# Fifteen list scatters in each attention pass and eighteen in the drain pass, with 31 left for the shared tiles

## The reference

```
xn = layernorm(x);  q, k, v = split(xn @ w_qkv);  q, k = elu(q) + 1, elu(k) + 1
kv[t] = decay * kv[t-1] + k[t] * v[t];  ks[t] = decay * ks[t-1] + k[t]
x = x + ((q * kv) / max(sum_d(q * ks), 1e-6)) @ w_out
```

```
xn2 = layernorm(x);  logits = xn2 @ router_w.T + router_b;  top 4 of 32
x = x + sum_4 share_e * down_e(silu(gate_e(xn2)) * up_e(xn2)) + shared(xn2)
```

## Time and profile before

| | us |
|---|---|
| median of 3 executions | 738.56 (735.03 to 739.55) |
| the profiled execution | 739.91 |
| its span, first to last instruction | 737.8 |
| PE busy in the span | 607.2 (82%) |
| DVE busy | 478.2 (65%) |
| ACT busy | 463.4 (63%) |
| POOL busy | 439.0 (59%) |

### The profile page before, as it was taken

The page is one execution under the profiler, slowest core; times in us unless marked ns, Lnnn a source line. Parts: engine busy times, 40 slices in busy tenths (PEclk is TensorE's granted clock), DMA queues, the critical chain, the costliest instruction groups (busy, mean ns, idle before and its releaser), DMA issues.

```text
span 737.8 us, 15716 instructions
## 1 busy us (share of the span) xinstructions
PE 607.2 (82%) x4797; PEld 419.7 (57%) x4797; DVE 478.2 (65%) x1894; ACT 463.4 (63%) x1118; POOL 439.0 (59%) x367
## 2 busy tenths in 40 slices
PE   4999988898897825576999999999999999999100
PEld 2467656566564413354777776777776777777000
DVE  2469979898896615444766666666666666666063
ACT  2687757677664203455877777877777777878100
POOL 3122287687687573444038787778878778887400
PEclk9999999999999966888999999999999999999655
DMA  9865788888756663566558887888888888887799
GB/s 290 295 179 161 234 242 255 284 248 251 241 162 207 214 205 100 185 203 203 167 135 139 136 146 139 138 136 147 137 144 140 136 140 138 144 142 97 162 412 379
DMA packets 122419, 140.41 MB, mean 190 GB/s; under 512 B 23586, under 2 KB 111170, under 8 KB 121794
## 3 DMA queue, kind: packets, MB, share of 16 engines
q1 hardware_dynamic: 89776, 97.29, 44.0%
q0 software_dynamic: 29040, 38.68, 29.6%
q10 hardware_dynamic: 3522, 3.44, 1.5%
HBM read 79.19 MB, written 64.89 MB: 195 GB/s over the span
## 4 chain that ended last, share of the span: by engine, by line
PE 65%; DVE 11%; another core or an unknown queue 6%; issue 5%; DMA 4%; ACT 3%; SPq 2%; POOL 2%; ACTq 0%; POOLq 0%; DVEq 0%
PE psD L1250 13%; PE psQ L1217 13%; PE psK L1217 12%; PE psT L1188 6%; PE psK L1266 3%; PE psV L1266 3%; SPq L513 2%; PE psT L1237 2%; PE psV L1237 2%; DMA W<-acc_scratch 2%; PE psD L1310 2%; PE psQ L1266 2%; DVE W L878 2%; DVE stats L806 1%
## 5 line engine op out<-in xcount | busy, mean ns | idle before, releaser
L637 POOL DMA_INDIRECT acc_scratch<-arena x159 | 249.3, 1568 | 96.6 <-DMA acc_scratch<-arena 42.8
L585 POOL DMA_INDIRECT xlist_scratch<-list_row,dest x128 | 134.9, 1054 | 66.6 <-issue 34.2
L1041 DVE COPY arena<-psT 128x512 f16<-128x512 f16 x191 | 81.1, 425 | 111.1 <-PE psT L1188 73.9
L1250 PE MATMUL psD<-W,arena 128*128 (+1 forms) x955 | 137.8, 276 | 8.1 <-DVE arena L1037 8.1
L1217 PE MATMUL psQ<-W,arena 128*128 (+1 forms) x570 | 111.2, 332 | 23.5 <-DVE arena L1041 17.9
L1217 PE MATMUL psK<-W,arena 128*128 (+1 forms) x576 | 112.2, 332 | 6.6 <-issue 4.7
L1250 PEld LDWEIGHTS psD<-W,arena 128*128 128x128 f16 x955 | 86.4, 99 | 15.7 <-DVE arena L1037 8.3
L1217 PEld LDWEIGHTS psQ<-W,arena 128*128 128x128 f16 x570 | 51.1, 99 | 57.6 <-DVE arena L1041 18.0
L669 ACT ACTIVATE arena<-arena 128x192 f16<-128x192 f32 x191 | 69.2, 362 | 16.3 <-DVE arena L1065 5.1
L1188 PE MATMUL psT<-ident,arena 128*128 128x128 f16 x764 | 75.4, 222 | 3.1 <-issue 3.0
L1188 PEld LDWEIGHTS psT<-ident,arena 128*128 128x128 f16 x764 | 58.1, 99 | 33.6 <-issue 12.4
(11 more groups left out here) (174 smaller groups left out, 1090.1 us busy)
## 6 DMA issues: line engine op xcount, KB each, us to landing
arena<-xlist_scratch SPq DMA_DIRECT2D x159, 136.0 KB
W<-acc_scratch SPq DMA_DIRECT2D x24, 512.0 KB, 12.8
acc_scratch<-arena SPq DMA_DIRECT2D x16, 512.0 KB, 6.8
arena<-in_L_attn_x_dram SPq DMA_DIRECT2D x10, 512.0 KB, 5.3
arena<-in_L_ffn_down_w_dram SPq DMA_DIRECT2D x23, 192.0 KB
xlist_scratch<-pad_scratch SPq DMA_DIRECT2D x32, 136.0 KB
list_row<-xrow_scratch SPq DMA_DIRECT2D x32, 136.0 KB
acc_scratch<-arena SPq DMA_DIRECT2D x33, 128.0 KB, 8.0
```

Of the source, the lines that this page charges most:

```text
L585: nc.gpsimd.indirect_dma_start(xlist[:, :], bass.IndirectOffsetOnAxis(ap=dest[:, n:n + 1], axis=0), list_row[j % LISTS][:, :], None).then_ ...
L637: nc.gpsimd.indirect_dma_start(acc[t % ACCS][:, :], bass.IndirectOffsetOnAxis(ap=token[:, (t - NT) % DEEP:(t - NT) % DEEP + 1], axis=0), y ...
L1041: nc.vector.tensor_copy(xT[t % 2].rearrange("p s c t -> p (s c t)"), psX[t % 2]).then_inc(xT_done, 1)
L1250: last = nc.tensor.matmul(psY[u], aT[u][0:height, part], weights(t - 2, GUW + q * H, H, height), start=(n == 0), stop=(n == len(parts) - 1))
```

## The change

It moves ten scatters into passes 3 to 7, two for each, so that the drain pass begins with n = 79 in place of 69. The drain pass does eighteen in place of twenty, and 31 in place of 39 are left. In the order of POOL's pass, the group between the two roots grows from four to five, and the group behind the second root from five to six; all others keep their size. `FETCHED` becomes 1, 2, 6, 10, 14, 17, 21, 26 for b = 2 to 9, before it was 1, 2, 6, 9, 12, 15, 19, 24. In the shared tiles SP therefore loads row tiles 26 and 27 at tiles 0 and 2, where it loaded 24 to 27 at tiles 0, 2, 5 and 7; the last four come at tiles 10, 12, 15 and 17 as before. No tile loads anything at 5 and 7 now.

```diff
-        LIST_FROM = [0, 0, 0] + [4 + 13 * n for n in range(NB - 2)] + [89]
+        LIST_FROM = [0, 0, 0] + [4 + 15 * n for n in range(NB - 2)] + [97]
...
+        def late_list(t):
+
+            j = NT - TS + (t - 10) // 5 * 2 + t % 5 // 2 if t >= 10 else FETCHED[NB + 1] + t // 5 * 2 + t % 5 // 2
+            return j if t % 5 in (0, 2) and j < (NT if t >= 10 else NT - TS) else None
...
-                if t % 5 in (0, 2) and FETCHED[NB + 1] + t // 5 * 2 + t % 5 // 2 < NT:
-                    load_list(FETCHED[NB + 1] + t // 5 * 2 + t % 5 // 2)
+                if late_list(t):
+                    load_list(late_list(t))
...
                 if b >= 3:
-                    list_some(2, 6)
+                    list_some(2, 7)
                 if st.now:
                     k_sum_product(b)
                 if st.before:
                     root(1, b - 1)
                 if b >= 3:
-                    list_some(6, 11)
+                    list_some(7, 13)
                 if st.now:
                     kv_sum_product(b, 0)
                 if b >= 3:
-                    list_some(11, 12)
+                    list_some(13, 14)
                 if st.now:
                     kv_sum_product(b, 1)
-                list_some(12 if b >= 3 else 0, 20)
+                list_some(14 if b >= 3 else 0, 20)
```

## The result

The kernel after takes 738.19 us (median of 20 runs, 733.23 to 746.2), the kernel before on the same chip 736.04 us (20 runs, 727.5 to 743.82). The ratio is **1.0075, interval 1.0043 to 1.0106**. It compares only executions within 1.5% of the fastest of their kernel, here 19 of after's and 12 of before's, while the medians of all twenty differ by 0.29%, so the size of the loss on this chip is less sure than the interval looks. The forecast was 732.6 us. On another chip, where before takes 683.47 us, after takes 692.23: **1.0135, interval 1.0101 to 1.0168**.

A forecast was written before the change was run, and what follows sets the result against it. Bounds: waits through DVE, PE and ACT in the passes, and holes on scatter trains in the shared tiles. 7.1 - 3.8 - 9.3 = -6.0 us from 739.91 gave 733.9; allowing for its 1.35 above the median, 732.6 us, range 724 to 744.

The forecast's parts named there:

- Second root, 4 x 0.5 us: Passes 4 to 7: one more scatter ahead of the second root makes normalization 0.5 us late each, 2.0 us.
- Pass 3, +1.3: Pass 3: DVE already waits for the root, so the added scatter's whole issue counts, 1.3 us.
- Before the first q * kv product ... nothing, with 1.2 us left: Passes: two more scatters, 2.54 us, fit POOL's idle 3.26 us, which grows by 0.5, and cost nothing.
- almost a pass of slack: Passes: SP's added list load and 272 KB more per pass stand behind loads with this slack and cost nothing.
- Price of a scatter: POOL: 0.96 us at the median, one each 1.27 us in a train, longest in a pass 1.97 us.
- The longer train beside the router, 3.8 us: Passes 4 to 7: six scatters behind the second root delay the logits, +1.0 in passes 4 to 6, +0.8 in 7.
- Holes, -3.8 and -9.3: Shared tiles: the first hole, at tile 0, ends 3.8 us earlier; losing the second, at tile 8, gives 9.3 us.
- The reading that trains do this: Shared tiles: PE's completions come late or crawl while POOL issues scatters back to back; holes end soon after their trains.
- the rival that the holes are not the scatters': Tiles 0 and 8: PE is stopped by something of its own, both holes stay; 745.7 us, chance 0.13.
- gated passes: Passes: the router waits for the end of the train each time; +12.7 - 13.1, 738.2 us, chance 0.15.
- The bound of +12.7 for the passes: Passes together: the highest cost, 5 x 2.54 = +12.7 us, where +7.1 was forecast.
- the sign of being wrong that the prediction named: The forecast is wrong if tile 8 still stalls, or passes grow by less than 0.5 or more than 2 us each.

The follow-up runs named there:

- the two kernels with fourteen: Fourteen scatters a pass, lists loaded early, the added one behind or ahead of the second root, against before at 684 us: 1.0019 and 1.0043.
- Fourteen ahead of the root: Fourteen scatters a pass, lists loaded early, the added one ahead of the second root, against before: 688.47 us, 1.0043.
- seven scatters: After with both moved scatters behind the second root and lists loaded early, against before: 0.9965 and 1.0006 at 684 us, 1.0195 at 737 us.
- lists early: After with SP loading later lists right behind the payload's store, against before: 738.51 us, 0.9973, and 737.53 us, 1.006.
- experiment 6: Before with POOL held at n = 76 until tile 1's gate: 1.0106; before with power operations between scatters n = 78 to 99: 739.3 and 707.66 us.
- the kernel with the tiles' part alone: Before with 28 scatters in the drain pass, 31 left, and after's list loads, against before: 0.9919 at 738 us, 1.0113 at 683 us.

## Why the prediction was wrong, step by step

- **Second root, 4 x 0.5 us: right in size.** 0.45 us a pass, by the two kernels with fourteen.
- **Pass 3, +1.3: the root's share is right, the pass is not.** Fourteen ahead of the root cost 1.28 us there, but after's pass 3 grew by 6.0 and 6.2. The rest goes with the list wait.
- **"Before the first q * kv product ... nothing, with 1.2 us left": the step that failed outright.** I set POOL's idle time against two more issues of 1.27 us, and put the list loads at nothing ("almost a pass of slack") without asking when each moved scatter needs its own. With 15 a pass, the first scatter of row tile 4 (n = 16) and of row tile 19 (n = 76) moved to the front of the product, ahead of their list, which SP loads only behind the stores and six pads. POOL stands idle there for 5.08 and 3.74 us, and for 6.31 and 1.36 on the chip at 683 us, which also waits 2.33 us in pass 4 between the two products (n = 32). The claim of idle time was thin as well: at 684 us the fifteenth scatter costs 0.7 us a pass with no wait at all.
- **Price of a scatter: right.** The Trainium skill's rule on the shared port (page "SBUF — State Buffer", section "Who interferes with whom") would have made the moved ones long, had they met it; no run shows that they did. Shortest, median and longest of after are within 5 ns of before's:

```profile
L590 POOL DMA_INDIRECT xlist_scratch<-list_row,dest x128: 954/962/1962, 92.3 to 348.9; - x128
```

- **The longer train beside the router, 3.8 us: as read from transposes to logits, right; what follows from it was missing.** Passes 4 to 7 have 1.0, 1.2, 0.6 and 0.1 us more of it than before, 2.9 in all, for a forecast of 3.8. At 684 us there is none of it. With seven scatters it is 8.9 us for passes 3 to 7, and in pass 6 ACT alone waits 5.00 us.
- **PE's clock: a term that I did not have.** Before's passes run at a granted clock of 1.00 and after's at 0.84 to 0.91. In pass 4 it falls to 0.57 behind PE's wait of 3.12 us for the split rows, is back within 4 us, and falls again for some ten us behind the waits in the router. The wait of 3.12 us isn't the price of the later root alone, for which PE waits 1.4 us (fourteen ahead). It comes where the root is later still. From the end of the list wait (123.47) to the root of pass 4 (142.45) POOL never stands idle for over 0.5 us, so the wait is handed on, and normalization waits 4.28 us for that root, where with lists early it waits 0.55 at most. What the low clock costs the passes is not shown by itself.
- **Holes, -3.8 and -9.3: right.** Tile 0 comes 4.4 us sooner behind the drain's logits, and from there to tile 9 it is 8.8 us less. The first hole ended with its train, and tile 8's is gone; the pitch from tile 3 to 11 is 2.2 us. The other 6 us of the -19.1, at tiles 17 to 19, had no term. The reading that trains do this held in experiment 6, and the rival that the holes are not the scatters' fell.
- **The sum:** in the profiled pair the passes cost 11.4 us more than forecast (+18.5 for +7.1) and the tiles gave back 6.0 more (-19.1 for -13.1), so that -6.0 became -0.6. That after's median, 738.19, equals the 738.2 of the rival "gated passes" (chance 0.15) is luck: that rival had +12.7 and -13.1, and no wait for a list. The bound of +12.7 for the passes was passed too (+22.5 at the first product of pass 7), and the sign of being wrong that the prediction named, passes growing by more than 2 us each, is what happened: 2.8 to 6.0.

## What to carry to other kernels

Before work is moved ahead in a queue, ask of each moved instruction which load it needs and when that load is issued in its own queue: an idle slot is only free for work that is ready. A long train of indirect scatters has a price that depends on the chip; keep it away from places where two engines pass work to and fro, or put other work between the scatters. And if moving the same 128 scatters about changes stages by 19 us and the whole by 1%, look for what decides (here POOL's 128 x 1.27 = 163 us of issue and the times at which SP can load the lists) before moving them again.

## What had not been expected of the hardware

- The same kernel takes 683 to 685 us on two chips and 737 to 739 on three. Nearly all of it lies ahead of tile 32: in the kernel before its first matmul is at 318.00 us on one and 373.17 on the other.
- The engines behind PE waited long for what PE's records show as done: ACT 21.6 us for the gate of tile 0 in before, 17.2 in after, 24.4 in the kernel with the tiles' part alone, only at 737 us and beside trains. The Trainium skill, page "SBUF — State Buffer", section "Who interferes with whom", says of the SBUF ports that PE and ACT never wait on anyone. These are waits for a semaphore, which that sentence does not speak of, and no run here shows a wait of PE for a port.
- Scatters that start every 2.4 us in place of 1.27 made no late signal from tile 0 to tile 12, on a chip where the train behind them did.
